# Attention queries carried in PSUM by ScalarE, and running maxima by one scan

## The chip, the cores and the metric

The kernel runs on one core of a Trainium2 chip. The metric is the device time of one launch in microseconds (us). Engines are named as in the profile: PE is TensorE (PEld its weight loads), DVE is VectorE, ACT is ScalarE, POOL is GpSimd and SP is SyncE. `L1310` is line 1310 of the kernel.

## The reference, cut to what matters

A small graph network: 6,250 nodes of 256 features, 200,000 edges, two layers. The change touches only the attention over the edges in the second layer, with 8 heads of 32:

```
q = (h @ Wq + bq).reshape(n, HEADS, HEAD_DIM) * scaling
k = (h @ Wk + bk).reshape(n, HEADS, HEAD_DIM)
v = (h @ Wv + bv).reshape(n, HEADS, HEAD_DIM)
s = jnp.einsum('ehd,ehd->eh', q[row], k[col])
m = jax.ops.segment_max(s, row, num_segments=n)
p = jnp.exp(s - m[row])
denom = jax.ops.segment_sum(p, row, num_segments=n)
attn = p / denom[row]
out = jax.ops.segment_sum(attn[:, :, None] * v[col], row, num_segments=n)
```

`row` is the edge's source node and `col` its target. Before this come layer norms, sums of edge attributes and a mixture of experts; behind it the output projection and a second mixture of experts.

## The kernel before

The program runs in stages that follow each other: the edges are sorted, edge attributes are summed per node, `node_stage` computes the node features with q, k and v, `attention` makes the weighted sums, and `output_stage` finishes. In the profiled execution attention takes the stretch from about 4,310 to 6,812 us.

In `attention` each of 128 partitions walks its own list of RP = 428 rows of S = 4 edge slots. All edges of one node lie next to each other, so a row either begins a new node or goes on with the node of the row before it in its partition. Nodes are kept apart by masks: `reset[:, k]` is 0 where row k goes on and very negative where it begins a node, and `goes[:, k]` is 1 or 0 in the same cases. The rows are worked in B2 = 107 batches of RB = 4 rows, which makes SB = 16 slots in a batch.

What each engine does in a batch, in the order of its program:

- **POOL** gathers keys and values of the 16 slots, one indirect DMA for each slot (L1153), into a ring of RING2 = 3 buffers. Before the gathers of batch b it waits for `s_sum`, the count of rows whose weighted values PE has summed, to reach the last row of batch b-3.
- **SP** loads the batch's query rows from HBM (L1175), which hold a query only where a row begins a node, and stores the states (L1185).
- **PE** builds the query row of every row in PSUM, AHEAD = 6 rows ahead of the row whose values it sums (`query_row`): a product with the identity puts down the loaded row (L1295, `start=True`) and a second adds the row that ACT has carried (L1296, `start=False`). Banks 4, 5 and 6 hold two query rows each and are used in turn; before a bank is used again PE waits for DVE's products of three pairs ago (`s_prod`). Then it sums the four weighted value slots of a row by four products with the identity into bank 0, 1, 2 or 3 (L1310), and counts `s_sum`. The profile shows each of these fp32 products as two MATMUL records. PE's batch b starts when DVE has finished `update(b - 1)` (`s_upd`).
- **ACT** carries (`carry`): it reads the query row of row k-1 in PSUM, multiplies it by `goes[:, k]` and writes it into SBUF, `carried` (L1327). It also takes the exponentials of the scores (L1335, into bank 7, `prob`) and of the drop of the maxima (L1336, `alpha`), and copies the maxima into the state (L1339). The order in a batch is L1335, L1336, L1339 and four carries.
- **DVE** multiplies the keys by the query rows (L1230, 4 of them), reduces over the 32 features (L1235), adds the padding mask (L1236), takes each row's maximum over its four slots (L1238, into `rowmax`), makes the running maximum of each row out of the row before (L1241, four in a chain), subtracts (L1243, L1244, L1246), runs `update(b - 1)`, and multiplies the values by `prob` (L1252, 4 of them). `update` takes four pairs: the state of the row before times `alpha` (L1208), and the sum from PSUM added to it (L1213), for which it waits on `s_sum`.

So a steady batch on DVE goes L1252 x4, L1230 x4, L1235, the small ones, L1208/L1213 x4. I call T the moment at which the last L1213 of an `update` ends; POOL, PE and SP turn to their next batch about then.

## Time and profile before

| what | value |
|---|---|
| time, median of 3 runs | 7474.96 us (7473.81 to 7492.86) |
| the profiled execution's own time | 7489.44 us |
| its span | 7487.7 us |
| granted TensorE clock, mean | 0.695 of full |
| busy over the span | PE 46%, PEld 36%, DVE 63%, ACT 9%, POOL 48% |
| attention stage | about 4310 to 6812 us |

The profiled execution took 14.5 us longer than the median. The stages follow one another, so the shares of the whole span say little of any one of them: what the change is worth has to be read within attention.

### The profile page before, as it was taken

To read this page: it belongs to the slowest core of one execution; us is meant where nothing else is said; L and a number is where in the kernel's file an instruction comes from. 1 tells how busy PE (TensorE), PEld (TensorE's weight loads), DVE (VectorE), ACT (ScalarE), POOL (GpSimd) and SP (SyncE) were. 2 spreads that over 40 slices of the span, in tenths; PEclk is the share of its full clock that TensorE was granted. 3 is DMA by queue.
4 is the path that set the end of the run, shared out by engine and by line. 5 is a ranking of instruction groups with operands and counts; after the bars stand their busy time and mean duration, and the time that the engine had idled before them with its cause. 6 is when DMAs were issued, how large, how long until landed. Compare 5 with 4: busy or idle time off the path is not lost. (4 is left out here: it accounts for less than half of the span.)

```text
span 7487.7 us, 44287 instructions
## 1 busy us (share of the span) xinstructions
PE 3459.1 (46%) x14187; PEld 2662.2 (36%) x14187; DVE 4682.8 (63%) x8349; ACT 660.4 (9%) x1436; POOL 3568.2 (48%) x3561
## 2 busy tenths in 40 slices
PE   0113332332010006666667745555555555554598
PEld 0113232221010004444444534444444444444465
DVE  9865555556878723333333367888888888885433
ACT  0000000000000001111111100111011111111122
POOL 0026666666777761111110066666666666663000
PEclk9555555555555557877788867777777777776699
DMA  0014433333223331111110067777777777773100
GB/s 9 0 45 137 138 133 128 130 127 121 93 92 94 105 121 25 42 42 42 42 42 30 21 210 221 237 234 234 234 233 236 235 234 234 232 236 99 43 15 20
DMA packets 339345, 925.83 MB, mean 124 GB/s; under 512 B 84356, under 2 KB 123505, under 8 KB 338854
## 3 DMA queue, kind: packets, MB, share of 16 engines
q0 software_dynamic: 198384, 588.63, 27.2%
q1 hardware_dynamic: 140194, 332.38, 12.3%
q8 instruction: 112, 1.84, 0.1%
q10 hardware_dynamic: 532, 1.98, 0.1%
q14 instruction: 123, 1.01, 0.0%
HBM read 662.99 MB, written 259.74 MB: 123 GB/s over the span
## 5 line engine op out<-in xcount | busy, mean ns | idle before, releaser
L479 POOL DMA_INDIRECT big<-in_edge_attr,big x1568 | 1620.5, 1034 | 1132.5 <-POOLq L321 478.2
L1153 POOL DMA_INDIRECT big<-keys_values,idx x1712 | 1636.7, 956 | 820.6 <-issue 494.4
L1310 PE MATMUL bank<-big,ident 128*128 128x264 f32 x3424 | 972.7, 435 | 18.7 <-DVE big L1252 10.0
L662 PE MATMUL bank<-big 128*128 128x64 bf16 x3200 | 426.8, 302 | 891.2 <-DVE big L529 663.9
L1310 PEld LDWEIGHTS bank<-big,ident 128*128 128x128 f32 x3424 | 757.2, 221 | 177.8 <-issue 19.6
L1295 PE MATMUL bank<-big,ident 128*128 128x256 f32 x854 | 331.1, 476 | 1056.2 <-DVE big L1213 998.8
L644 DVE SCALAR_TENSOR_TENSOR big<-big 128x128 f32<-128x128 f32 x1567 | 555.6, 355 | 261.2 <-DMA big<-in_edge_attr,big 209.3
L662 PEld LDWEIGHTS bank<-big 128*128 128x128 bf16 x3200 | 368.6, 147 | 949.2 <-DVE big L529 701.5
L854 POOL DMA_INDIRECT queries_by_row<-big,firstrow x49 | 48.0, 979 | 1234.6 <-DVE big L959 1221.8
L528 DVE TENSOR_TENSOR big<-big 128x1024 bf16<-128x1024 bf16 x400 | 276.0, 690 | 575.2 <-remote 488.3
L1295 PEld LDWEIGHTS bank<-big,ident 128*128 128x128 f32 x854 | 183.5, 232 | 1133.6 <-DVE big L1213 1042.3
L1230 DVE TENSOR_TENSOR big<-big,bank 128x1024 f32<-128x1024 f32 x428 | 496.1, 1215 | 58.3 <-DMA big<-keys_values,idx 23.7
L1252 DVE TENSOR_TENSOR big<-big,bank 128x1056 f32<-128x1056 f32 x428 | 508.1, 1249 | 5.0 <-issue 0.3
L940 DVE SCALAR_TENSOR_TENSOR big<-bank,big 128x256 f32<-128x256 f32 x392 | 158.7, 477 | 531.0 <-PE bank L996 531.0
L1235 DVE TENSOR_REDUCE big<-big 128x128 f32<-128x4096 f32 x107 | 473.0, 4420 | 3.6
L244 PE MATMUL bank<-ident,big 128*128 128x128 f32 x224 | 51.2, 423 | 904.8 <-DVE big L197 488.0
L1327 ACT ACTIVATE big<-bank,goes 128x256 f32<-128x256 f32 x427 | 202.5, 474 | 2211.9 <-remote 889.6
L1213 DVE TENSOR_TENSOR big<-big,bank 128x264 f32<-128x264 f32 x428 | 183.6, 429 | 319.9 <-remote 301.4
L996 PE MATMUL bank<-big 128*128 128x256 f32 x1568 | 364.1, 392 | 22.0 <-DVE big L940 22.0
L983 PE MATMUL bank<-big 128*128 128x448 f32 x896 | 373.1, 572 | 0.7 <-ACT big L1083 0.7
L244 PEld LDWEIGHTS bank<-ident,big 128*128 128x128 f32 x224 | 45.8, 227 | 909.2 <-issue 594.1
L179 DVE TENSOR_TENSOR big<-big 128x1024 f32<-128x1024 f32 x294 | 360.4, 1226 | 10.1
(341 smaller groups left out, 5074.4 us busy)
## 6 DMA issues: line engine op xcount, KB each, us to landing
running_sums<-big SPq DMA_DIRECT2D x196, 512.0 KB
running_attention<-big SPq DMA_DIRECT2D x107, 544.0 KB
queries_by_row<-big SPq DMA_DIRECT2D x107, 512.0 KB
big<-queries_by_row SPq DMA_DIRECT2D x107, 512.0 KB
big<-keys_values,idx POOLq DMA_INDIRECT x1712
big<-in_edge_attr,big POOLq DMA_INDIRECT x1568
keys_values<-big SPq DMA_DIRECT2D x7, 1820.0 KB
x_after_layer<-big SPq DMA_DIRECT2D x7, 896.0 KB
```

Of the source, the lines that this page charges most:

```text
L179: v.tensor_tensor(dst[:, :, 0, :], src[:, :, 0, :], src[:, :, 1, :], ALU.min)
L479: pool.indirect_dma_start(out=z.rows[:, r, k, :], out_offset=None, in_=w["edge_attr_128"][:, :], in_offset=bass.IndirectOffsetOnAxis(ap=z. ...
L644: scan.then(v.scalar_tensor_tensor(out=z.rows[:, r, k, :], in0=before, scalar=z.goes1[:, c:c + 1], in1=z.rows[:, r, k, :], op0=ALU.mult, o ...
L662: mm = pe.matmul(bank[4 + k][:, 0:64], lhsT=z.oh_lo[:, r, :, j], rhs=z.oh_hi[:, r, :, j], start=False, stop=True, skip_group_check=True)
L983: mm = pe.matmul(bank[2 * f + h][:, 0:CN // 2], lhsT=w1[:, k, e, f * P:(f + 1) * P], rhs=tT[:, k * CN + h * CN // 2:k * CN + (h + 1) * CN ...
L996: mm = pe.matmul(bank[4 + b // 2][:, (b % 2) * D:(b % 2 + 1) * D], lhsT=hT[:, e % 2, k, b * P:(b + 1) * P], rhs=w2[:, k, e, :], start=(k = ...
L1153: pool.indirect_dma_start(out=kv[:, r, k, :], out_offset=None, in_=t["kv"][:, :], in_offset=bass.IndirectOffsetOnAxis(ap=m.idx2[:, c:c + 1 ...
L1230: ins = v.tensor_tensor(row, row, query(b, i).unsqueeze(1).to_broadcast([P, S, D]), ALU.mult)
L1235: sc.then(v.tensor_reduce(own, keys.rearrange("p c (h d) -> p c h d", d=HD), AX.X, ALU.add))
L1252: v.tensor_tensor(values, values, prob[:, i * S:(i + 1) * S].unsqueeze(3).to_broadcast([P, S, HEADS, HW]), ALU.mult).then_inc(s_val, 1)
L1295: pe.matmul(query(b, i), lhsT=m.ident[:, :], rhs=qr[:, b % RING2, i], start=True, stop=False, skip_group_check=True)
L1310: mm = pe.matmul(weighted(i), lhsT=m.ident[:, :], rhs=kv[:, b % RING2, i * S + j, D:KW], start=(j == 0), stop=(j == S - 1), skip_group_che ...
```

## The change

ACT now writes the carried row straight into the PSUM place of query row k, and PE adds the loaded row to it with one product (`start=False`). The second product and the SBUF tile `carried` are gone. The wait for DVE's products of three pairs ago moves from PE to ACT, since ACT is now the first to write a bank. For row 0 ACT copies the first queries into the bank. Before all that PE writes zeros into banks 4 to 6 once, with three 128x512 products of a zeroed tile.

On DVE the four chained maxima are one scan of 128x40: per head one leading element, which is reset by a very negative number and takes the maximum brought over from the last batch, and four rows. The maxima now lie head by head (stride 5), so the row maxima are written, and the maxima read, with a stride. ACT has one more small copy in a batch (the last maximum of each head into `fresh`), for which DVE waits before its scan (`s_first`). DVE's setup for the stage has two more memsets (128x1024 and 128x856) and a copy of the resets into the new layout (128x3424).

```diff
@@ attention @@
+    peak, at = cut(m.big, at, 2, HEADS, RB + 1)
+    fresh, at = cut(m.big, at, HEADS, RB + 1)
+    breaks, at = cut(m.big, at, B2, HEADS, RB + 1)
-    carried, at = cut(m.big, at, 2, D)
-    rowmax, at = cut(m.big, at, RB, HEADS)
...
+    nothing = state[:, RING2 - 1, RB - 1, 0:D]
@@ vector: setup @@
-            st.add(v.memset(peak[:, 0:HEADS], -BIG))
+            st.add(v.memset(fresh[:, :, 0], -BIG))
+            st.add(v.memset(each, 0.0))
+            st.add(v.memset(breaks[:, :, :, 0], -3.0 * BIG))
+            st.add(v.tensor_copy(breaks[:, :, :, 1:RB + 1], m.reset[:, :].rearrange("p (b r) -> p b r", r=RB).unsqueeze(2)
+                                 .to_broadcast([P, B2, HEADS, RB])))
@@ vector: batch @@
-                        dve.wait_ge(s_car, min(b * RB + i + 2, RP - 1))
+                        dve.wait_ge(s_car, min(b * RB + i + 3, RP))
...
-                mx.then(v.tensor_reduce(rowmax, slots.rearrange("p r j h -> p r h j"), AX.X, ALU.max))
-                for i in range(RB):
-                    k = b * RB + i
-                    mx.then(v.scalar_tensor_tensor(out=maxima(k + 1, 1)[:, 0], in0=maxima(k, 1)[:, 0], scalar=m.reset[:, k:k + 1],
-                                                   in1=rowmax[:, i], op0=ALU.add, op1=ALU.max))
+                mx.then(v.tensor_reduce(fresh[:, :, 1:RB + 1].rearrange("p h r -> p r h"), slots.rearrange("p r j h -> p r h j"),
+                                        AX.X, ALU.max))
+                if b:
+                    dve.wait_ge(s_first, b)
+                mx.then(v.tensor_tensor_scan(peak[:, h].rearrange("p h r -> p (h r)"), breaks[:, b].rearrange("p h r -> p (h r)"),
+                                             fresh.rearrange("p h r -> p (h r)"), -BIG, ALU.add, ALU.max))
@@ tensor: query_row @@
-                if k % 2 == 0 and k >= 6:
-                    pe.wait_ge(s_prod, k // 2 - 2)
-                if k == 0:
-                    pe.wait_ge(s_q0, 16)
-                    mm = pe.matmul(query(b, i), lhsT=m.ident[:, :], rhs=q0, start=True, stop=True, skip_group_check=True)
-                else:
-                    pe.wait_ge(s_car, k)
-                    pe.matmul(query(b, i), lhsT=m.ident[:, :], rhs=qr[:, b % RING2, i], start=True, stop=False, skip_group_check=True)
-                    mm = pe.matmul(query(b, i), lhsT=m.ident[:, :], rhs=carried[:, k % 2], start=False, stop=True,
-                                   skip_group_check=True)
+                pe.wait_ge(s_car, k + 1)
+                loaded = qr[:, b % RING2, i] if k else nothing
+                mm = pe.matmul(query(b, i), lhsT=m.ident[:, :], rhs=loaded, start=False, stop=True, skip_group_check=True)
                 mm.then_inc(s_qry, 1)
 
+            for k in range(4, 7):
+                mm = pe.matmul(bank[k][:, :], lhsT=m.ident[:, :], rhs=each[:, 0:4, :].rearrange("p h n -> p (h n)"), start=True,
+                               stop=True)
+            mm.then_inc(s_clear, 1)
@@ scalar: carry @@
                     act.wait_ge(s_qry, k)
-                    a(carried[:, k % 2], query((k - 1) // RB, (k - 1) % RB), ACT.Copy, scale=m.goes[:, k:k + 1]).then_inc(s_car, 1)
-
+                    if k % 2 == 0 and k >= 6:
+                        act.wait_ge(s_prod, k // 2 - 2)
+                    a(query(k // RB, k % RB), query((k - 1) // RB, (k - 1) % RB), ACT.Copy, scale=m.goes[:, k:k + 1]).then_inc(s_car, 1)
+
+            act.wait_ge(s_q0, 16)
+            act.wait_ge(s_clear, 1)
+            a(query(0, 0), q0, ACT.Copy).then_inc(s_car, 1)
             carry(0, AHEAD)
@@ scalar: batch @@
-                a(state[:, r, :, HEADS * HW:SW], maxima(b * RB + 1, RB), ACT.Copy).then_inc(s_peak, 1)
+                a(state[:, r, :, HEADS * HW:SW], maxima(b, 1, RB), ACT.Copy).then_inc(s_peak, 1)
+                if b + 1 < B2:
+                    a(fresh[:, :, 0], peak[:, h, :, RB], ACT.Copy).then_inc(s_first, 1)
```

How PE's rows stand in a steady batch, before (two query products, then the four value products of a row, each written as one row with its count):

```order
L1310 MATMUL bank<-big,ident 128x264 x4
L1295 MATMUL bank<-big,ident 128x256
L1296 MATMUL bank<-big,ident 128x256
L1310 MATMUL bank<-big,ident 128x264 x4
L1295 MATMUL bank<-big,ident 128x256
L1296 MATMUL bank<-big,ident 128x256
```

and at the start of the stage and in the first batch now (L1301 clears the banks, L1297 is the query product, L1314 the values):

```order
L1290 MATMUL bank<-ident,big 128x128
L1301 MATMUL bank<-big,ident 128x512 x3
L1297 MATMUL bank<-big,ident 128x256 x7
L1314 MATMUL bank<-big,ident 128x264 x4
L1297 MATMUL bank<-big,ident 128x256
L1314 MATMUL bank<-big,ident 128x264 x4
```

The order is the same; one of every two query products is gone, and three products stand ahead of the first query row.

ACT's program in a steady batch before, with the waits that stand in a row (`queries_ready` is `s_qry`, `products_ready` is `s_prod`):

```order
L1335 ACTIVATE bank<-big 128x128 [waits values_ready,differences_ready]
L1336 ACTIVATE big<-big 128x32
L1339 ACTIVATE big<-big 128x4x8 [waits states_stored0]
L1327 ACTIVATE big<-bank,goes 128x256 [waits queries_ready] x4
L1335 ACTIVATE bank<-big 128x128 [waits values_ready,differences_ready]
```

and now:

```order
L1350 ACTIVATE big<-big 128x8
L1333 ACTIVATE bank<-bank,goes 128x256 [waits queries_ready]
L1333 ACTIVATE bank<-bank,goes 128x256 [waits products_ready,queries_ready]
L1333 ACTIVATE bank<-bank,goes 128x256 [waits queries_ready]
L1333 ACTIVATE bank<-bank,goes 128x256 [waits products_ready,queries_ready]
L1344 ACTIVATE bank<-big 128x128 [waits values_ready,differences_ready]
L1345 ACTIVATE big<-big 128x32
```

Every second carry has a further wait, for DVE's products, and behind the last of them stands the exponential of the next batch.

## Rows read from the trace of the kernel before

**Rows 1.** Windows: us, busy PE PEld DVE ACT POOL (records), clock, DMA share

```profile
4392.70:6755.90 2363.20, 1348.41 (x4944) 1090.94 (x4944) 1985.56 (x2678) 242.23 (x721) 1575.87 (x1649) 0.77 0.76 233
```

**Rows 2.** Groups of instructions: count, busy us, mean ns, idle before, releasers

```profile
L1153 POOL DMA_INDIRECT big<-keys_values,idx x1712 | 1636.7, 956 | 820.6 <-issue 494.4 <-remote 298.7 <-PE bank L1310 27.6
L1213 DVE TENSOR_TENSOR big<-big,bank 128x264 f32<-128x264 f32 x428 | 183.6, 429 | 319.9 <-remote 301.4 <-PE bank L1310 7.4
L1296 PE MATMUL bank<-big,ident 128*128 128x256 f32 x854 | 306.6, 446 | 0.0
```

**Rows 3.** Timeline, one steady batch: start us, us, engine, [idle before <-releaser]

```profile
5510.94 1.94 PE L1310 MATMUL bank<-big,ident 128*128 128x264 f32 x8
...
5517.83 0.97 POOL L1153 DMA_INDIRECT big<-keys_values,idx  x1 [0.30 <-issue]
...
5520.81 0.47 ACT L1327 ACTIVATE big<-bank,goes 128x256 f32<-128x256 f32 x1 [11.48 <-remote]
...
5521.72 0.43 DVE L1213 TENSOR_TENSOR big<-big,bank 128x264 f32<-128x264 f32 x1 [2.82 <-remote]
5521.89 0.95 POOL L1153 DMA_INDIRECT big<-keys_values,idx  x1 [3.09 <-remote]
...
5522.21 1.22 PE L1295 MATMUL bank<-big,ident 128*128 128x256 f32 x2 [9.32 <-DVE big L1213]
...
5544.56 0.43 DVE L1213 TENSOR_TENSOR big<-big,bank 128x264 f32<-128x264 f32 x1 [3.03 <-remote]
```

**Rows 4.** Windows view, two stretches of that batch

```profile
5513.00:5519.00 6.00, 0.00 (x0) 0.00 (x0) 5.42 (x17) 0.00 (x0) 4.58 (x5) 0.67 0.76 204
5521.60:5522.20 0.60, 0.00 (x0) 0.00 (x0) 0.44 (x2) 0.12 (x2) 0.31 (x1) 0.50 0.00 0
```

**Rows 5.** Timeline, batch 1, which began at 4392.70

```profile
4402.04 1.94 PE L1310 MATMUL bank<-big,ident 128*128 128x264 f32 x8
...
4415.03 0.43 DVE L1213 TENSOR_TENSOR big<-big,bank 128x264 f32<-128x264 f32 x1 [2.99 <-remote]
```

**Rows 6.** Timeline, the long batch; windows view, it and its three neighbours

```profile
4503.46 0.43 DVE L1213 TENSOR_TENSOR big<-big,bank 128x264 f32<-128x264 f32 x1
...
4510.92 1.94 PE L1310 MATMUL bank<-big,ident 128*128 128x264 f32 x8
...
...
4543.49 0.43 DVE L1213 TENSOR_TENSOR big<-big,bank 128x264 f32<-128x264 f32 x1
...
4484.09:4585.10 101.01, 55.43 (x192) 43.84 (x192) 77.12 (x104) 9.55 (x28) 61.55 (x65) 0.75 0.69 212
```

**Rows 7.** Timeline, last update, after the last gather

```profile
6807.25 0.43 DVE L1213 TENSOR_TENSOR big<-big,bank 128x264 f32<-128x264 f32 x1 [0.93 <-PE bank L1310]
```

**Rows 8.** Timeline of the four maxima; source view of the only scan

```profile
5514.01 1.06 DVE L1241 SCALAR_TENSOR_TENSOR big<-big,reset 128x8 f32<-128x8 f32 x4
L540 DVE TENSOR_TENSOR_SCAN big<-big x1: 416/416/416, 1814.7 to 1814.7; 64x128 f32<-64x128 f32 x1
```

**Rows 9.** Groups: ACT's carry and exponential, DVE's products with queries and weights

```profile
L1327 ACT ACTIVATE big<-bank,goes 128x256 f32<-128x256 f32 x427 | 202.5, 474 | 2211.9 <-remote 889.6 <-PE bank L1296 780.6 <-issue 541.7
L1335 ACT ACTIVATE bank<-big 128x128 f32<-128x128 f32 x107 | 29.4, 274 | 59.3 <-issue 40.0 <-DVE big L1246 19.2
L1252 DVE TENSOR_TENSOR big<-big,bank 128x1056 f32<-128x1056 f32 x428 | 508.1, 1249 | 5.0 <-issue 0.3 <-ACT bank L1335 0.2
L1230 DVE TENSOR_TENSOR big<-big,bank 128x1024 f32<-128x1024 f32 x428 | 496.1, 1215 | 58.3 <-DMA big<-keys_values,idx 23.7 <-ACT big L1327 18.2 <-remote 8.5
```

**Rows 10.** Timeline, start of the stage

```profile
4323.39 1.19 PE L1292 MATMUL bank<-big,ident 128*128 128x256 f32 x2 [3.40 <-DMA big<-queries,q0idx]
...
4341.07 4.61 DVE L1230 TENSOR_TENSOR big<-big,bank 128x1024 f32<-128x1024 f32 x4 [20.36 <-DMA big<-keys_values,idx]
```

**Rows 11.** Groups: the nearest rows to the added setup on DVE

```profile
L1442 DVE COPY big<-big 128x1792 f32<-128x1792 f32 x7 | 7.7, 1094 | 0.2
L577 DVE MEMSET big<- 128x2048 int32 x1 | 1.8, 1765 | 0.5 <-issue 0.5
```

More of the change, by code:

```diff
@@ L762, in node_stage @@
              "hidden_ready", "expert_products", "expert_added", "x2_ready", "qkv_products", "qkv_read",
-             "node_steps", "x2_kv_stored", "kv_ready", "q_scattered", "bias_added", "node_consts")
+             "node_steps", "x2_kv_stored", "kv_ready", "q_scattered", "bias_added")
     s = {n: sem(n) for n in names}
@@ L1095, in attention @@
     state, at = cut(m.big, at, RING2, RB, SW)
-    peak, at = cut(m.big, at, (RP + 1) * HEADS)
+    peak, at = cut(m.big, at, 2, HEADS, RB + 1)
+    fresh, at = cut(m.big, at, HEADS, RB + 1)
+    breaks, at = cut(m.big, at, B2, HEADS, RB + 1)
     score, at = cut(m.big, at, 2, SB, HEADS)
-    carried, at = cut(m.big, at, 2, D)
-    rowmax, at = cut(m.big, at, RB, HEADS)
     drop, at = cut(m.big, at, 2, RB, HEADS)
@@ L1113, in attention @@
     s_st = [sem(f"states_stored{r}") for r in range(RING2)]
-    s_set, s_q0 = sem("attention_set"), sem("first_queries")
+    s_clear, s_q0 = sem("query_banks_cleared"), sem("first_queries")
     s_car, s_qry, s_prod, s_sco, s_max = sem("queries_carried"), sem("queries_ready"), sem("products_ready"), sem("score_steps"), sem("maxima_steps")
-    s_diff, s_prob, s_alpha, s_peak = sem("differences_ready"), sem("weights_ready"), sem("decays_ready"), sem("maxima_copied")
+    s_diff, s_prob, s_alpha = sem("differences_ready"), sem("weights_ready"), sem("decays_ready")
+    s_peak, s_first = sem("maxima_copied"), sem("last_maxima_copied")
     s_val, s_sum, s_upd, s_tmp = sem("values_ready"), sem("sums_ready"), sem("states_ready"), sem("update_steps")
@@ L1126, in heads, with maxima @@
         return x.rearrange("p (h w) -> p h w", w=HW)
-    def maxima(first, count):
-        return peak[:, first * HEADS:(first + count) * HEADS].rearrange("p (r h) -> p r h", h=HEADS)
+    def maxima(b, first, count):
+        return peak[:, b % 2, :, first:first + count].rearrange("p h r -> p r h")
     def weighted(i):
@@ L1237, in _ @@
                 slots = own.rearrange("p (r j) h -> p r j h", j=S)
-                mx.then(v.tensor_reduce(rowmax, slots.rearrange("p r j h -> p r h j"), AX.X, ALU.max))
-                for i in range(RB):
-                    k = b * RB + i
-                    mx.then(v.scalar_tensor_tensor(out=maxima(k + 1, 1)[:, 0], in0=maxima(k, 1)[:, 0], scalar=m.reset[:, k:k + 1],
-                                                   in1=rowmax[:, i], op0=ALU.add, op1=ALU.max))
-                sc.add(v.tensor_tensor(slots, slots, maxima(b * RB + 1, RB).unsqueeze(2).to_broadcast([P, RB, S, HEADS]), ALU.subtract))
-                mx.then(v.tensor_tensor(drop[:, h], maxima(b * RB, RB), m.reset[:, rows].unsqueeze(2).to_broadcast([P, RB, HEADS]),
+                mx.then(v.tensor_reduce(fresh[:, :, 1:RB + 1].rearrange("p h r -> p r h"), slots.rearrange("p r j h -> p r h j"),
[4 more added lines that the diff above has]
+                                             fresh.rearrange("p h r -> p (h r)"), -BIG, ALU.add, ALU.max))
+                sc.add(v.tensor_tensor(slots, slots, maxima(b, 1, RB).unsqueeze(2).to_broadcast([P, RB, S, HEADS]), ALU.subtract))
+                mx.then(v.tensor_tensor(drop[:, h], maxima(b, 0, RB), m.reset[:, rows].unsqueeze(2).to_broadcast([P, RB, HEADS]),
                                         ALU.add))
-                v.tensor_tensor(drop[:, h], drop[:, h], maxima(b * RB + 1, RB), ALU.subtract).then_inc(s_diff, 1)
+                v.tensor_tensor(drop[:, h], drop[:, h], maxima(b, 1, RB), ALU.subtract).then_inc(s_diff, 1)
                 if b:
@@ L1261, in _ @@
             st.wait()
-            mine = maxima(RP, 1)[:, 0]
+            mine = peak[:, (B2 - 1) % 2, :, RB]
             st.then(v.tensor_reduce(gmax, each, AX.X, ALU.max))
@@ L1315, in _ @@
                 tr = pe.transpose(bank[2 + h // 4][:, (h % 4) * P:(h % 4 + 1) * P],
-                                  peak[:, RP * HEADS + h:RP * HEADS + h + 1].to_broadcast([P, P]), m.ident[:, :])
+                                  peak[:, (B2 - 1) % 2, h, RB:RB + 1].to_broadcast([P, P]), m.ident[:, :])
             tr.then_inc(s_mturned, 1)
```

## The prediction

> **What bounds the kernel now.** I read the windows view first. In the attention stretch, 2363.20 us for 103 batches (1,649 gathers at 16 a batch), a batch takes 2363.20 / 103 = 22.94 us, in which PE is busy 13.1 us, DVE 19.3 us and ACT 2.4 us [rows 1]. POOL's 15.3 us of busy time leave out the 0.30 us between two gathers: one every 0.95 + 0.30 = 1.25 us makes 20.1 us for 16 [rows 2, 3]. No engine fills the 22.9 us, so something is waited for in every batch. The groups name it: L1213 idles 301.4 us on "remote" and POOL's L1153 298.7 us on "remote", some 3 us in each of about 100 batches [rows 2].
>
> The timeline of one batch shows what "remote" is. L1213, the last of an update, starts at 5521.72 after 2.82 us of waiting, and POOL's first gather at 5521.89 after 3.09 us [rows 3]. In the code both wait for the same event, the batch's last `s_sum` from PE. Yet PE's last products started at 5510.94 and took 1.94 us [rows 3], so they ended at 5512.88, and PE did no matmul between 5513 and 5519 [rows 4]. The count was seen almost 9 us later. ACT's last carry was held up likewise: 11.48 us idle, to 5520.81 [rows 3]. When the signal came, DMA traffic had just stopped (share 0.00 behind 5521.60; it was 0.76 from 5513 to 5519) [rows 4]; POOL's last gather had been issued at 5517.83 [rows 3].
>
> So I read the loop as follows: POOL issues 16 gathers (20.1 us with the last one's tail), their data lands about 3 us later, only then does PE's last count of the batch get through, and DVE and POOL go on together. T to T is 5544.56 - 5521.72 = 22.84 us [rows 3]. How PE's signal and the gather traffic hang together no row tells; that they do, three rows say. In batch 1 PE's last products ended at 4403.98, 11.3 us into the batch, and L1213 still started only at 4415.03, 22.3 us in, after 2.99 us of waiting [rows 5]: the wait did not move with PE's end. In the long batch POOL had run without a pause, PE's products ended at 4512.86 and the update only at 4543.92, 40.0 us after the one before [rows 6]. And with no gathers left the row names PE's L1310 itself, after 0.93 us [rows 7].
>
> **The change, part by part.**
>
> PE loses one query product of two, 446 ns a record, two records a product [rows 2]: 4 x 2 x 0.446 = 3.6 us busy in a batch; since records overlap their successors, I count 306.6 / 427 = 0.72 us each, 2.9 us a batch at most. PE would then end some 2 to 3 us earlier, at about 10 us after T in place of 12 to 13. PE idles 9.32 us before its next batch [rows 3], so by the reading above this is worth 0; if the cover were gone it would be worth up to 3 us a batch.
>
> The Trainium skill speaks against my reading of these rows: "Perfetto Trace Analysis", section "Per-instruction lifecycle: what the profiler-reported window actually captures", says that the end of a TensorE instruction is an estimate and not an observation. If PE in truth ended 9 us later than its rows say, PE would be what is waited for; that is rival A.
>
> DVE loses four chained maxima, 1.06 us with their gaps, and gets one scan of 128x40 [rows 8]. The scan lies between one of the four removed (1.06 / 4 = 0.27 us, 8 elements) and the scan of 128 elements, 416 ns [rows 8]; nearer the former, 0.3 us. Strided maxima in four small instructions may cost 0 to 0.3 us. So DVE gains 0.4 to 0.7 us a batch. Its new wait for `s_first` is for an ACT copy made right behind the exponentials at the end of the batch before, while the scan takes the place of L1241, which began at 5514.01, 14.7 us after T: 0. The 2.82 us wait [rows 3] hides the gain: DVE reaches L1213 earlier and waits longer. It counts only in the handful of batches where DVE does not wait there (428 rows give 107 updates, of which about 102 wait), 5 x 0.6 = 3 us.
>
> The Trainium skill, "DVE: opcode table, instruction layouts, handler registers and perf-mode slots", section 6, says that the scan runs at half throughput; the 416 ns row shows it no worse than 3.3 ns an element, overhead included. Over 40 elements that changes nothing.
>
> ACT's carry reads PSUM in 474 ns and now writes PSUM also; the exponential with a PSUM output took 274 ns [rows 9], so no penalty is seen, and I take 0, with 0.1 us as the upper end. One more copy is 0.27 us at most. Each carry is in the row-to-row chain, but ACT is busy 2.4 us in 22.9 [rows 1]: 0. The moved wait: the fourth carry of a batch now needs DVE's first pair of products of the next batch. DVE has made them 4 x 1.25 + 2 x 1.2 = 7.4 us after T [rows 9]. The carry's own query row is the one that PE puts down just ahead of the last value products, 11.6 us after T before (5510.94 against T = 5499.31) [rows 3] and some 9 us after it now. The wait is over before it is reached: 0. Queued behind it stand L1344 and L1345, on which L1259 and the next update wait; were the products late, each microsecond would go to DVE.
>
> At the start of the stage DVE's setup grows by memsets of 1024 and 856 columns and a copy of 3424. By 1765 ns for 2048 the memsets take 1.6 us; by 1094 ns for 1792 the copy takes 2.1 us, and at twice that for its stride and broadcast 4.2 [rows 11]: 3.7 to 5.8 us. PE then clears three banks; by 1.22 us for 256 columns [rows 3], 2.4 us for each of 512, 7.3 in all, or half that at a higher clock. PE was idle from 4323.39 - 3.40 = 4319.99 [rows 10], so clearing ends at 4320 + 5.8 + 7.3 = 4333.1 at the latest. A row step afterwards is 1.22 + 0.47 and a tenth for the hops, 1.8 us; two rows and the carries bring the first pair to 4333.1 + 4.1 = 4337.2, ahead of 4341.07, where DVE's first products start when the gathers have come after 20.36 us of idleness [rows 10]. So 0; if both prices were 50% too low, the first pair would come at 4343.8, 3 us late.
>
> **Sum**, against the profiled execution's own 7489.4 us: PE 0, DVE -3, ACT 0, start 0: 7486.4. The median of the runs is 14.5 us lower, so for it this gives 7475.0 - 3 = 7472. Both ends of the costs: -0.3 us in each of 103 batches, if DVE's and POOL's restart after the signal tighten (-31), to +3 at the start and +0.1 a batch (+14): 7441 to 7489 us.
>
> **Rivals.**
>
> A. PE is the one waited for. Its ends are late in truth, or the last count slips out early when PE is done earlier. Then the 3 us wait goes, and POOL's 20.1 us and DVE's 19.3 - 0.6 are next: the batch falls from 22.85 to 20.1, 100 x -2.7 = -270, 7205 us. For it: the skill's rule, and that "remote" is not a transfer of this kernel's own. Against it: batch 1, where PE ended over a microsecond earlier than in the steady batch and nothing moved, and the granted clock, which is at 0.50 (1.2 GHz) by 5521.6, after PE had done nothing for 8 us [rows 4, 5]. Chance 0.12.
>
> B. On the other side: the earlier end takes away the pause. If the last count gets through before POOL has finished, POOL starts its next 16 gathers without a gap, and every following signal meets an unbroken stream, as in the long batch of 40.0 us. It decides when the count comes over 2.2 us earlier than now (22.3 us after T, less POOL's 20.1). The long batch and its neighbours, two of them short, took 101.0 us in four, 25.25 each [rows 6], so one such event costs 101.0 - 4 x 22.85 = +9.6 us. If the pattern fills the stage, 103 x 2.4 = +247: 7722 us. If one to ten more come, +10 to +96: 7482 to 7568. For it: it did happen, once. Against: 100 batches of 107 keep their pause. Chance 0.10 for some, 0.08 for all.
>
> C. The change does not do on DVE what it says: the scan and the strided reads cost more than the four they replace. To lengthen a batch they must cost over 2.8 us more than what they replace, seven times the known scan. Chance 0.02, and with 1 us over that, +100 us: 7575.
>
> **How the numbers follow.** My forecast, nothing but a few microseconds, has 0.68, C 0.02, A 0.12, some long batches 0.10, all 0.08. Its own range is 7441 to 7489. The range of all leaves out A and the full B, 0.20: so 7440 to 7580, which holds C too. Changes under 0.3% (22 us), about what a measurement can tell from none, are "same". Of my own case 0.67 is within it and 0.01 beyond it to the fast side; of the partial B one or two events stay within it, 0.04. Faster: A and 0.01, 0.13. Same: 0.71. Slower: 0.06 + 0.08 + 0.02 = 0.16.
>
> **What would show it.** In the profile after: L1297 half as many records as L1295 and L1296 had together, PE's last L1314 ending 10 to 11 us after T, and the last L1219 still starting 22.3 us after T, with a "remote" sum of 301 + 100 x 0.6 = about 360 us on it and again 299 on POOL's gathers. PE idle ahead of L1297 12 us in place of 9.3. L1248 about 0.3 us, 107 times. The first L1236 still at 17 us or so into an idle stretch that the gathers end. Right for A: POOL's "remote" under 50 us and T to T at 20.1. Right for B: more than one batch of about 40 us. Wrong for my costs: L1344 ending an idle stretch of L1259, or L1333 waiting on DVE's L1236.

## The result

The changed kernel takes 7537.71 us (median of 11 runs, 7488.01 to 7580.82), the kernel before in the same job 7484.39 (11 runs, 7472.82 to 7498.94). The ratio is 1.0065, interval 1.0042 to 1.0089: 0.65% slower, and its runs spread over 93 us where those of before spread over 26. The profiled execution's span is 7537.3 us, 49.6 more than before.

The groups of instructions in the changed kernel's profile, as in [rows 2, 8, 9]:

```profile
L1155 POOL DMA_INDIRECT big<-keys_values,idx x1712 | 1630.2, 952 | 892.6 <-issue 496.5 <-remote 224.2 <-PE bank L1314 171.8
L1297 PE MATMUL bank<-big,ident 128*128 128x256 f32 x856 | 355.1, 505 | 1215.9 <-DVE big L1219 807.6 <-ACT bank L1333 222.2 <-issue 185.0
L1236 DVE TENSOR_TENSOR big<-big,bank 128x1024 f32<-128x1024 f32 x428 | 493.8, 1211 | 260.6 <-ACT bank L1333 194.7 <-remote 37.2 <-issue 26.0
L1219 DVE TENSOR_TENSOR big<-big,bank 128x264 f32<-128x264 f32 x428 | 183.4, 428 | 250.5 <-remote 225.1 <-PE bank L1314 12.5 <-issue 0.8
L1248 DVE TENSOR_TENSOR_SCAN big<-big 128x40 f32<-128x40 f32 x107 | 25.9, 242 | 3.7
L1333 ACT ACTIVATE bank<-bank,goes 128x256 f32<-128x256 f32 x427 | 191.3, 448 | 2030.5 <-PE bank L1297 802.4 <-remote 779.5 <-issue 448.6
```

The wait ahead of L1219 has shrunk (250.5 us against 319.9 on L1213 before), but another has grown, ahead of DVE's products with the queries: 260.6 us, 194.7 of them ended by ACT's carry, where L1230 had idled 58.3 [rows 9]. The scan and the carry cost what they should.

Where these waits lie shows when the stage is cut into batches, from the end of one update to the end of the next. Batches 5 to 14 of the changed kernel took, in us (from the ends of its rows for L1219): 19.2, 33.6, 20.0, 22.8, 22.8, 22.8, 19.2, 38.3, 19.2, 20.8. Before there was one such long batch in 107 [rows 6]; now there are 14 over 30 us. The windows view of three neighbours (columns as in [rows 1]) and of the middle of the long one:

```profile
4614.40:4633.60 19.20, 11.15 (x40) 8.54 (x40) 18.70 (x24) 2.48 (x8) 14.48 (x16) 0.77 0.80 249
4633.60:4671.90 38.30, 13.51 (x40) 9.93 (x40) 18.85 (x23) 2.48 (x8) 20.35 (x22) 0.68 0.58 176
4671.90:4691.10 19.20, 11.44 (x41) 8.71 (x41) 18.70 (x24) 2.39 (x8) 12.62 (x14) 0.77 0.76 242
4641.00:4658.00 17.00, 0.09 (x1) 0.00 (x0) 1.30 (x2) 0.00 (x0) 10.22 (x11) 0.64 0.70 206
```

In the last window ACT does nothing, PE and DVE next to nothing; only POOL's gathers run. The timeline tells how it comes to that:

```profile
4614.16 0.94 POOL L1155 DMA_INDIRECT big<-keys_values,idx  x1 [2.97 <-remote]
...
4615.56 0.94 POOL L1155 DMA_INDIRECT big<-keys_values,idx  x1 [0.46 <-issue]
...
4623.76 1.94 PE L1314 MATMUL bank<-big,ident 128*128 128x264 f32 x8
...
4633.16 0.43 DVE L1219 TENSOR_TENSOR big<-big,bank 128x264 f32<-128x264 f32 x1
...
4634.57 0.94 POOL L1155 DMA_INDIRECT big<-keys_values,idx  x1 [0.31 <-issue]
...
4639.15 1.94 PE L1314 MATMUL bank<-big,ident 128*128 128x264 f32 x8
...
4653.33 0.95 POOL L1155 DMA_INDIRECT big<-keys_values,idx  x1 [0.30 <-issue]
4659.13 0.45 ACT L1333 ACTIVATE bank<-bank,goes 128x256 f32<-128x256 f32 x1 [21.25 <-remote]
4659.68 2.35 DVE L1236 TENSOR_TENSOR big<-big,bank 128x1024 f32<-128x1024 f32 x2 [17.38 <-ACT bank L1333]
...
4666.13 0.94 POOL L1155 DMA_INDIRECT big<-keys_values,idx  x1 [11.86 <-PE bank L1314]
```

PE's last products of the first batch end at 4625.70, 11.3 us into it. The trace's own record of that semaphore has its last step at 4631.82: 6.1 us late, but with the gathers still running (in the steady batch of [rows 3] it has it at 5521.63, 8.75 us late and behind them). So the last L1219 starts at 4633.16 without a wait (before: after 2.82 us, [rows 3]). POOL, when it has issued its 16 gathers, goes on at 4634.57 after its ordinary 0.31 us; the pause of 3 us is missing. In the batch that follows, PE's second query row is done at 4639.31 (the value products behind it at 4641.09), and ACT sees its count only at 4659.13, after the last gather of that stream (issued at 4653.33). ACT's carry waits, DVE's products wait for the carry, PE for both. This is rival B of the prediction.

The sum: batches 1 to 105 took 809.6 + 799.7 + 798.0 = 2407.3 us before (by thirds) and 810.9 + 827.6 + 834.8 = 2473.3 now, +66.0. The stage's first update ends 10.4 us earlier than before (4382.2 against 4392.7) and what lies behind the last batch is 6 us shorter: +49.6 in all. A whole group of four (19.2 + 38.3 + 19.2 + 20.8 = 97.5) costs 6.5 us more than four of 22.76.

Where the long batches lie is not chance: all 14 have a number that six divides (6, 12, 24, 36 and so on to 102), and so has the only one before, batch 6. The batch ahead of each, 5, 11, 23 and so on, is the one in which the count came early. In that batch POOL's stream has a small irregularity: ahead of its second gather stand 0.45 us and not 0.30 (the row at 4615.56). It comes once in 96 gathers, 16 times in the stage, before and now alike; the table at the end of the experiments uses it.

### The profile page after: what moved, and what is told of

Same layout as the page of the kernel before. It is cut to its first block and busy times, and to the rows that moved or that the text cites. A ratio compares the mean times of both kernels' runs of the same rounds, so it can differ in the third digit from the quotient of the medians.

```text
span 7537.3 us, 42697 instructions
## 1 busy us (share of the span) xinstructions
PE 3338.6 (44%) x13339; PEld 2496.0 (33%) x13339; DVE 4625.1 (61%) x8031; ACT 671.6 (9%) x1543; POOL 3557.5 (47%) x3561
## 5 line engine op out<-in xcount | busy, mean ns | idle before, releaser
L1314 PE MATMUL bank<-big,ident 128*128 128x264 f32 x3424 | 1051.6, 461 | 25.6 <-DVE big L1259 10.3
L1297 PE MATMUL bank<-big,ident 128*128 128x256 f32 x856 | 355.1, 505 | 1215.9 <-DVE big L1219 807.6
L1314 PEld LDWEIGHTS bank<-big,ident 128*128 128x128 f32 x3424 | 782.8, 232 | 262.3 <-DVE big L1259 69.3
L1236 DVE TENSOR_TENSOR big<-big,bank 128x1024 f32<-128x1024 f32 x428 | 493.8, 1211 | 260.6 <-ACT bank L1333 194.7
L1297 PEld LDWEIGHTS bank<-big,ident 128*128 128x128 f32 x856 | 194.8, 247 | 1305.2 <-DVE big L1219 846.0
L1333 ACT ACTIVATE bank<-bank,goes 128x256 f32<-128x256 f32 x427 | 191.3, 448 | 2030.5 <-PE bank L1297 802.4
L179 DVE TENSOR_TENSOR big<-big 128x1024 f32<-128x1024 f32 x294 | 360.3, 1225 | 10.1
L180 DVE TENSOR_TENSOR big<-big 128x1024 f32<-128x1024 f32 x294 | 358.0, 1218 | 0.0
```

What stands on the lines that cost most here:

```text
L179: v.tensor_tensor(dst[:, :, 0, :], src[:, :, 0, :], src[:, :, 1, :], ALU.min)
L1236: ins = v.tensor_tensor(row, row, query(b, i).unsqueeze(1).to_broadcast([P, S, D]), ALU.mult)
L1297: mm = pe.matmul(query(b, i), lhsT=m.ident[:, :], rhs=loaded, start=False, stop=True, skip_group_check=True)
L1314: mm = pe.matmul(weighted(i), lhsT=m.ident[:, :], rhs=kv[:, b % RING2, i * S + j, D:KW], start=(j == 0), stop=(j == S - 1), skip_group_che ...
```

## Experiments

The runs were made in seven jobs, six of which are on record with their chip's number, all different (that of the result is not known), and this turned out to matter. In two jobs (the first and third below) the kernel before took 6990 us; in the five others, that of the result among them, 7479 to 7527. I call the latter chips that hold the counts, for the reason given with the first job. No chip is known to have been met twice, so the chip is not told apart here from a state it was in at the time.

### Each part alone, a padded PE and a shorter one

Four kernels. The queries alone: `maxima` and its four chained instructions as before. The scan alone: `query_row` and `carry` as before. The other two:

```diff
 e3_pe_padded: behind the query product of a row, for k >= AHEAD
+    pe.matmul(bank[3][:, HEADS * HW:HEADS * HW + 248], lhsT=m.ident[:, :], rhs=<zeros of each, 248 columns>, start=True, stop=True)
 e5_pe_shorter: in the sum of a row's values
-                    for j in range(S):
+                    for j in range(S - 1):
```

> The part on the queries alone (ACT writes the carried rows into PSUM, PE one product a row, clearing of the banks); the four chained maxima and their layout are those of before. Theory (the gap is lost: PE ends 1 to 2 us earlier, its last count of the batch sometimes gets through while gathers still run, POOL starts the next 16 without a pause, and the batch after that takes about 38 us): five or more batches of over 30 us, +20 to +80 us. Rival (the scan and its shorter DVE path bring it about): one such batch as before, time within 0.3% of before.

> The scan alone, queries as before (two products, carried through SBUF). Theory: PE's end in a batch stays at 12 to 14 us, so one or two long batches as before, and a time within 0.3% of before. Rival (DVE's part brings it about): five or more long batches, +20 to +80 us.

> The changed kernel, and PE gets one further product of 128x248 of zeros a row, into columns of bank 3 that nobody reads, in the place of the product that the change took away. Theory: PE's last products of a batch end at 12 to 14 us again, the count is held until the gathers have landed, long batches go back to one or two, time within 0.3% of before (7470 to 7500). Rival (the direct write by ACT or the moved wait is at fault, not PE's earlier end): five or more long batches stay, 7520 or more.

> The changed kernel with three value products a row in place of four (the sum leaves out the fourth slot of each row), so that PE ends another 1.9 us earlier. Theory: the last count gets through early in more batches, and long batches come more often, every three to five batches: 15 to 30 of them, 7600 to 7730. Rival (PE's end is what the batch waits for, and its rows only tell it too early): the period falls by 1.9 us in most batches, 7300 to 7350.

Measured: before 6989.69 (31 runs); 6994.93, 6989.49, 6991.64 and 6990.96 us, ratios 1.0010, 1.0005, 1.0007 and 1.0003, none further than 0.2% from before by its interval. No batch over 30 us in any. The groups of the first of them show the reason:

```profile
L1155 POOL DMA_INDIRECT big<-keys_values,idx x1712 | 1632.8, 954 | 521.7 <-issue 521.7
L1216 DVE TENSOR_TENSOR big<-big,bank 128x264 f32<-128x264 f32 x428 | 183.4, 428 | 18.0 <-PE bank L1310 3.3
```

"Remote" is gone. On this chip PE's counts come at once, although the same gathers run: the record of the semaphore has a step 0.01 to 0.02 us behind the end of every product that counts, where on its holding chip the kernel before shows only 280 steps for 428 counts, and the last of a batch some 9 us late. POOL never pauses, and a batch takes POOL's 20.1 to 20.2 us on average (706.1 us for 35 of them), with PE's work and DVE's under it. All four expectations were made for a chip that holds the counts and were not tested. What this does show: neither the kernel nor the stream of gathers by itself holds them; the chip, or its state at the time, has a part in it. PE's recorded ends are also shown to be good by it.

The three repeats in the third job met another chip of the same kind: 6993.43, 6987.92 and 6995.38 us beside 6990.61. The padded kernel as a whole was not run on a holding chip; it was there only as a third of the stage, below.

> The part on the queries alone, once more, hoping for a chip on which the kernel before takes about 7480 us. There, theory (PE's earlier end lets the last count through now and then, POOL's pause is lost, the next batch takes about 38 us): five or more batches over 30 us, +20 to +80 us. Rival (the scan brings it about): one such batch, within 0.3%. On a chip with 6990 us it tells nothing new: within 0.3%.

> The scan alone, once more. At 7480 us, theory: one or two batches over 30 us, within 0.3% of before. Rival: five or more, +20 to +80 us. At 6990: within 0.3%.

> The changed kernel with one further product of zeros a row, once more. At 7480 us, theory: PE ends at 12 to 14 us after T as before, one or two batches over 30 us, within 0.3% of before. Rival (ACT's direct write or the moved wait is at fault): five or more stay, +20 to +80 us. At 6990: within 0.3%.

### The changed kernel once more

> The changed kernel itself, unaltered, beside the kernel before, on whatever chip this job gets. On the chip of the four runs above the kernel before took 6990 us, not 7480, POOL never waited for PE's count and a batch took 19.2 to 20.1 us. Theory (the loss needs a chip on which PE's counts are held up while gathers run): where the kernel before takes about 6990, the changed one is within 0.3% of it and has no batch over 30 us; where before takes about 7480, it is 30 to 70 us slower with six or more batches over 30 us. Rival (the loss belongs to the changed kernel on any chip): 0.65% slower at 6990 also, about 7035.

Measured: 7530.4 us against 7478.57, ratio 1.0072 (1.0050 to 1.0095), with nine batches over 30 us in the profile (2, 6, 8, 24, 26, 50, 78, 96, 102). The loss is reproduced on a holding chip. The changed kernel itself was not run where the counts are not held; there only its parts were, and they make no difference.

### Three ways in one kernel

To be independent of the chip I put the ways to build a query row into one kernel, by thirds of the stage.

```diff
 mix_a: MODES = ("two", "one", "padded"); mix_b: ("padded", "two", "one"); thirds: b < 36, b < 71, rest
+    two:    PE puts down the loaded row and adds `carried`; ACT carries into SBUF; PE waits for s_prod
+    one:    as in the changed kernel
+    padded: as one, and the product of zeros of e3_pe_padded
```

> One kernel with three ways to build the query rows, so that they meet the same chip: batches 0 to 35 as before (two products a row, carried through SBUF), 36 to 70 as in the changed kernel, 71 to 106 as changed with one further product of zeros a row. The maxima by scan throughout. On a chip where POOL's count is held up (before at about 7480 us), theory (PE's earlier end takes away POOL's pause): at most one batch over 30 us in the first third, two to five in the second, none or one in the last. Rival (scan on DVE at fault): two to five in each third. Rival (ACT's direct write or the moved wait at fault): two to five in the second and in the last third. On a chip where before takes about 6990 us: none anywhere.

> The same three ways in another order: padded, then as before, then as changed. Theory, on a chip with held counts: at most one long batch in each of the first two thirds, two to five in the last. Rivals as for the run before. At 6990: none.

Where one way gives over to another, a few rows of these two kernels get a query that is not the reference's; their instructions and waits are not changed by it. Each of these mixed kernels was executed once. The windows view by thirds (35 batches each), first of mix_a, then of mix_b:

```profile
4397.50:5202.70 805.20, 459.75 (x1680) 371.31 (x1680) 655.33 (x805) 86.80 (x280) 530.70 (x558) 0.78 0.76 232
5202.70:6031.00 828.30, 423.58 (x1400) 318.74 (x1400) 654.70 (x806) 86.11 (x280) 533.60 (x561) 0.73 0.73 226
6031.00:6827.10 796.10, 452.09 (x1672) 368.34 (x1672) 653.96 (x805) 83.01 (x276) 517.63 (x545) 0.77 0.74 229
```

```profile
4393.40:5203.70 810.30, 455.80 (x1680) 370.49 (x1680) 654.20 (x805) 84.35 (x280) 532.85 (x561) 0.77 0.75 231
5203.70:6003.60 799.90, 458.13 (x1680) 371.02 (x1680) 655.16 (x806) 86.62 (x280) 533.92 (x561) 0.78 0.76 234
6003.60:6829.70 826.10, 428.28 (x1396) 322.00 (x1396) 654.79 (x805) 84.38 (x276) 518.90 (x545) 0.73 0.71 220
```

The third with one product a row is the long one in both, 828 and 826 us against 796 to 810, and holds all the long batches but one: 1, 5, 0 in mix_a and 0, 0, 5 in mix_b. The padded third has everything of the change, ACT's write, the moved wait and the scan, except PE's earlier end (13.0 us behind T in the median, against 12.15 in the third with one product), and has no long batch. So of the parts of the change it is the removed product; that it acts by PE's end, and not merely by PE's smaller work, rests on the table at the end of the experiments. DVE's busy time is the same in all six.

### PE shorter yet, and half the gathers

```diff
 mix_c: thirds: as changed | sum over S - 1 slots | POOL gathers SB // 2 slots of a batch
```

> The changed kernel in the first third; in the second each row's sum leaves out its fourth slot, so that PE ends 1.9 us earlier yet; in the last third POOL gathers only 8 of the 16 slots of a batch (the others keep the rows of an earlier batch), 10 us of gathers and then a pause. On a chip with held counts, theory: two to five batches over 30 us in the first third, more (five to nine) in the second, and none in the last, where a batch takes DVE's 19.2 us. Rival (PE's rows tell its end too early, and its work is what the batch waits for): second third 1.9 us a batch shorter, last third unchanged at 22.8. At 6990: 19 to 20 us in all three.

```profile
4397.60:5201.10 803.50, 415.92 (x1400) 314.91 (x1400) 654.08 (x805) 86.39 (x280) 533.34 (x561) 0.72 0.76 233
5201.10:6034.40 833.30, 345.02 (x1120) 251.34 (x1120) 655.34 (x807) 85.41 (x280) 525.79 (x552) 0.71 0.71 221
6034.40:6706.10 671.70, 407.86 (x1396) 309.75 (x1396) 654.83 (x805) 85.29 (x276) 255.89 (x266) 0.77 0.51 161
```

In the second third PE was done at 10.6 us in its first batch, at 8.2 to 10.6 in the short batches that followed and at 17 to 30 in the long ones. Every second batch loses its pause: from batch 43 on they alternate between 19.2 and, mostly, 28.6 us, and the third takes 833 us although 70 us of PE's busy time are gone. The numbers of long batches missed what was expected: one over 30 us in the first third (batch 6; two to five expected) and four in the second (five to nine), most of whose long ones stay just under 30. With half the gathers, and PE's work as in the first third, each batch takes 671.7 / 35 = 19.2 us, DVE's own time. That the work of PE is what a batch waits for, its true end being later than its rows say (rival A), is out: then taking work from PE should have helped, and taking gathers away should not.

### A forced pause

```diff
 e6_pool_pause: POOL, before the gathers of batch b
+                if b:
+                    pool.wait_ge(s_g[(b - 1) % RING2], 16 * SB * ((b - 1) // RING2 + 1))
 mix_d: none | until all 16 | until 15 of 16 have landed (a second semaphore for the last gather)
 mix_e: as mix_d, and the sum over S - 1 slots;  mix_f: until 14 | 13 | 12 have landed
 v_early_paced: 15 of 16 throughout, and PE's first query row of a batch ahead of its wait for s_upd
```

> The changed kernel, and POOL waits before each batch's gathers until those of the batch before have landed, so that a pause of some 3 us in the gather stream is certain. At 7480 us, theory: no batch over 30 us, 22.2 to 22.9 us in every one, 7430 to 7480, that is 50 to 100 us faster than the changed kernel. Rival (the long batches have another cause than a missing pause): they stay, and the time is 7530 or more. At 6990, where POOL's 20.1 us set the batch, the pause costs 2 to 3 us in each: 7200 to 7310.

It ran on a chip that does not hold the counts: 7466.26 us against 6990.61, ratio 1.0688 (1.0666 to 1.0709), more than the 7200 to 7310 expected. The pause came out at 4 to 5 us, not 3, and a batch at 24.7.

> The changed kernel, with a forced pause in the gather stream by thirds: batches 0 to 35 none; 36 to 70 POOL waits until all 16 gathers of the batch before have landed; 71 to 106 until 15 of them have (a shorter pause). On a chip that holds PE's counts, theory (a missing pause makes the long batches): one to five batches over 30 us in the first third, none in the second at 22.8 to 24.5 us each; in the last third either none, or fewer than in the first. Rival (the long batches do not hang on POOL's pause): two to five in each third. On a chip that does not hold them: none; about 20, 24.3 and 21 to 23 us a batch.

> As the run before, and each row's sum leaves out its fourth slot, so that PE ends at about 10.6 us after T, early enough for its counts to get through in nearly every batch. Theory, on a holding chip: first third alternates short and long (19.2 and 28.7 us, as in the second third of the run with 7400 us), none over 25 us in the second (24 us each); in the last third, if a short pause is enough, 21 to 22 us in each batch, which would be below the 22.8 of the kernel before. Rival: a short pause does not clear what holds the counts, and the last third alternates as the first.

The thirds of mix_d, on a holding chip:

```profile
4373.00:5181.90 808.90, 411.90 (x1400) 312.38 (x1400) 654.18 (x806) 86.53 (x280) 530.50 (x558) 0.73 0.75 230
5181.90:6042.80 860.90, 410.64 (x1400) 309.10 (x1400) 658.22 (x805) 86.73 (x280) 530.96 (x557) 0.71 0.71 217
6042.80:6878.80 836.00, 401.18 (x1396) 304.23 (x1396) 656.97 (x805) 85.27 (x276) 524.60 (x551) 0.71 0.71 220
```

Long batches: 2, 0, 0; in mix_e 6, 0, 0 (830.1, 858.4 and 833.4 us). The evidence is mix_e: its first third alternates as expected, and with a forced pause and the same early end of PE no batch is over 26 us. The two of mix_d are batches 2 and 6, at the start of the stage, and the rest of its first third had none even without a forced pause. But the pause costs more than it saves: 24.6 us a batch for all 16, 23.9 for 15, against 22.8; the 21 to 22 us hoped for in mix_e's last third did not come.

> Whole function. The changed kernel; PE does the first query row of a batch ahead of its wait for DVE's update (some 1 us less behind T), and POOL waits before a batch until 15 gathers of the one before have landed. On a holding chip, if a short pause is enough and PE then ends before about 11 us after T: 21 to 22.5 us a batch, 7330 to 7450. If not: 22.8 and a few long ones, 7470 to 7560. On a chip that does not hold them it costs 1 to 3 us a batch: 7100 to 7300.

7560.3 us against 7484.67, ratio 1.0093 (1.0064 to 1.0123), no batch over 30 us, 23.9 us each. PE's end did not come earlier by it (11.9 us). The expected gain was wrong: waiting for the fifteenth gather makes a pause of 3.85 us (median), longer than the natural 3.0, so nothing could be won. Its groups show what took the place of "remote":

```profile
L1158 POOL DMA_INDIRECT big<-keys_values,idx x1712 | 1631.5, 953 | 916.1 <-issue 515.8 <-DMA big<-keys_values,idx 244.0 <-PE bank L1320 156.3
L1240 DVE TENSOR_TENSOR big<-big,bank 128x1024 f32<-128x1024 f32 x428 | 493.6, 1215 | 504.1 <-DMA big<-keys_values,idx 467.5 <-issue 36.6
L1222 DVE TENSOR_TENSOR big<-big,bank 128x264 f32<-128x264 f32 x428 | 183.5, 429 | 18.8 <-PE bank L1320 4.1
```

DVE now waits for the gathers themselves (467.5 us), and no longer for PE's count.

> The changed kernel; POOL waits before a batch until 14 (batches 0 to 35), 13 (36 to 70), 12 (71 to 106) gathers of the batch before have landed. With 15 the pause was 3.7 us and a batch took 23.9. One gather less should shorten the pause by 1.25 us each: 2.4, 1.2 and 0.3 us. On a holding chip: first third as the unforced one, 22.8 with fewer or no long batches; if a pause of 1.2 us were enough, the second third takes 21.4 to 22; in the last third the pause is gone and long batches come (two to five). Rival (a pause under 2.9 us never clears the counts): long batches in the second and last third.

813.5, 801.8 and 799.5 us, with 2, 0 and 0 long batches; the two long ones (batches 6 and 8) came behind pauses of 1.5 and 1.1 us, so a pause of that length was not enough there. The shorter pauses that were expected did not come. In the other two thirds the added wait was over long before the count: pauses stayed at 3.1 us in every batch. The long batches expected of the last third did not come either, although PE ended before 12.0 us in more than half of the batches. What this kernel's gather stream lacks is the gap of 0.45 us: it has none in the stage. A single execution took 7518.25 us beside a median of 7527.0, within the spread of before.

### Each part alone on a holding chip

> The part on the queries alone, for its time on a chip that holds PE's counts (before at about 7480 us). By the mixed kernels the loss is all here: five or more batches over 30 us, +20 to +80 us. At 6990: within 0.3%.

> The scan alone, for its time on such a chip: none or one batch over 30 us, within 0.3% of before, at the fast side by a few us if at all. At 6990: within 0.3%.

The kernel before took 7527.0 us here. The queries alone: 7583.3, ratio 1.0077 (1.0052 to 1.0102), nine batches over 30 us in the profile. The scan alone: 7530.62, ratio 1.0003 (0.9987 to 1.0018), one. The whole loss is in the part on the queries; the scan gains nothing that can be measured.

### What decides whether the pause is lost

From seven traces of holding chips (before, the changed kernel twice, mix_a, mix_b, each part alone) I took the batches 9 to 103 that follow an ordinary one of 22.6 to 23.4 us, and noted when PE's last products end after T, whether the batch took under 22.3 us, that is, whether the count got through early, and whether the gap of 0.45 us stands in its gather stream, which is the case in batches 11, 17, 23 and so on, every sixth:

```
                      batch with the 0.45 us gap     any other batch
PE's end after T      batches   through early        batches   through early
under 11.5 us            27        25                   45         2
11.5 to 12.0             22        12                   24         0
12.0 and later           57         0                  322         0
```

Two things have to come together. PE's end has to lie before about 12 us: before and with the scan alone, all ends in these batches lie at 12.0 or later, with one product a row half or more lie below. That it is the end, and not PE's smaller work as such, shows in the kernels and thirds with one product alone: in the batches with the gap 25 of 27 counts came early, then 12 of 22, and at 12.0 us and later none of 4. And of all 39 early counts 37 fall in the one batch of six whose stream has the gap. The same holds in stretches without the gap: in the first third of mix_d and in all of mix_f 74 ordinary batches ended before 12 us and one count was early, where mix_d's forced pause sets in (batch 35). In the first third of mix_c, with the gap, all five such ends lay close to 12 (11.8 and later), and none was early.

The limit of 12 us is that of the steady stretch alone. In batch 5, near the start of the stage, the count came early at an end of 12.6 us in the kernel before, 12.7 in mix_a and 12.4 with the scan alone. Nor is the gap needed when PE is earlier yet: the second third of mix_c began with an end of 10.6 us and an early count outside the sixth batches. Whether the gap itself lets the count through, or something else that comes once in 96 gathers, no run shows; none moved the gap.

## Why the prediction was wrong

**What bounds the kernel.** Right, on chips that hold the counts: gathers, landing, count, restart. The half-gather third (19.2 us) and the semaphore's own record bear it out. That it is a property of the chip as well could not be seen in one trace: on two others POOL's 20.1 us set the batch.

**PE's removed products, "worth 0".** This is the step that failed: an earlier end of PE was taken to cost nothing, and it cost the loss, +66.0 us over batches 1 to 105 in the profiled executions. In a wait that opens by the moment at which something arrives, an earlier arrival is not free. I leaned on batch 1, whose end at 11.3 us changed nothing. One batch could not tell: outside the sixth batches, ends under 11.5 us left the count held in 43 of 45 cases, and in the sixth ones in 2 of 27.

The size was wrong too. PE's end was to move from 12 to 13 us to about 10; it moved from 13.1 to 12.0 (median), and PE's busy time over those batches fell from 1373.1 to 1273.4 us, 0.95 us a batch and not 2.9. The 0.72 us counted for a removed product mixes both levels of the clock and overlaps its neighbours; at the full clock a row's period fell by 0.44 us (2.65 before, by the ends of the last two rows at 5510.24 and 5512.88; 2.21 now, 4623.49 and 4625.70). And with less work on PE the granted clock in this stretch was 0.73 in place of 0.77: 917 of the 3,360 value records took over 0.48 us, where 626 had. By mix_c and mix_e, an end at 10 us would have made the loss larger, not nil.

**The chances.** Rival B had its place, its sign and its signature right (more than one batch of about 40 us, the wait moved to the carry) and 0.18 in all. Against it I set that 100 of 107 batches kept their pause. That was the frequency at the old end of PE, and the change moves exactly that end; nothing in the rows of before lay between 11.3 and 12 us in the steady stretch. Its price of 9.6 us for each event was too high: a full one costs 6.5 with DVE's shorter batches, some (about 32 us) only 3. Thirteen more of them came, above the one to ten of its case "some"; that its 7482 to 7568 held the result is in part luck, since the count was too low and the price too high.

**DVE.** Right. The scan took 242 ns (0.3 expected), one strided subtract (L1250) 0.385 us against 0.294 for L1243, and batches that wait for nothing went from 19.81 to 19.16 us: 0.65 in place of 0.6. **ACT.** Right: the carry that writes PSUM took 448 ns against 474. **The start.** Clearing and setup were hidden; DVE's first product came 7.7 us earlier than before, at 4333.33 against 4341.07, and still behind an idle stretch of 15.48 us; why it came earlier no run shows. **The moved wait.** Right in the steady stretch, where it ends no idle time. At the start of the stage one carry (4335.77) waited 5.5 us for DVE's first pair of products (L1236 from 4333.33 on), and the first exponential stood behind it; the prediction had the wait over before it is reached. **Rival A.** Out by mix_c and mix_e, and by the record of the semaphore on the two other chips. **The signs.** L1297 had 856 records, half of the 1,708 of before, as forecast; the "remote" sum on L1219 was 225.1 us and not about 360, since the long batches took its place, and PE idled 807.6 us in all ahead of L1297 for DVE, less than the 998.8 before, not more.

## To carry to other kernels

When a wait ends by a release that does not follow the producer's last row, ask what releases it, and treat the distance between the two as something that a change can cross in either direction. An engine that ends earlier on a hidden path can start another engine earlier and take away a pause on which a third depends; the price is in the batches behind it, not in the one that got faster. Such a mechanism is tested best by putting the variants into thirds of one kernel, since then all meet the same chip; here two of seven jobs met chips on which the mechanism was not seen. And before rare events are called chance, list where they fall: here the places, every sixth batch, were in the first trace of the changed kernel.

## What the runs showed of the hardware

In five of seven jobs PE's semaphore counts were seen by DVE, ACT and POOL late while POOL's indirect gathers ran, often only after the stream's last gather had been issued: some 9 us late in a steady batch of the kernel before (5512.88 to 5521.63), 19.8 us in a long one of the changed kernel (4639.31 to 4659.13). Where the gathers were halved no batch waited for them (19.2 us). In the other two jobs every one was recorded 0.01 to 0.02 us behind the product's end, with the same gathers running. The kernel before took 7479 to 7527 us in the former and 6990 us in the latter. A pause of 3 us cleared them, one of 1.1 to 1.5 us did not in the two cases seen. In the seven holding traces of the table one gather in 96 is preceded by 0.45 us and not 0.30, and 37 of 39 early counts fall in the batch that has it; on the two other chips the same program shows no such gap. What path the counts share with the gathers, what the gap is, and in what the chips differ, stays open.
